# Attention's denominators: four sums an octet through a ring of four PSUM banks, instead of one accumulated sum in a bank of its own

## The reference

```python
attn = jax.nn.softmax(jnp.einsum('bhnd,bhmd->bhnm', q, k) * scale, axis=-1)
out = jnp.einsum('bhnm,bhmd->bhnd', attn, v)
out = out.transpose(0, 1, 3, 2).reshape(B, C, H, W)
out = conv1x1(out, wo, bo)
return (out + q_in) / jnp.sqrt(jnp.float32(2.0))
```

## Time and profile before

| | before |
|---|---|
| median of the runs shown | 5332.25 us |
| the profiled execution, its own time | 5332.55 us |
| its span, first to last instruction | 5330.8 us |
| PE busy | 5102.7 us, 96% of the span |
| DVE busy | 3992.7 us, 75% |
| POOL busy | 3101.9 us, 58% |
| ACT busy | 2791.8 us, 52% |
| mean granted clock of PE | 0.981 of full speed |

### The profile page before, as it was taken

One profiled execution on the slowest core, in us unless ns is written; L12 is line 12 of the kernel. 1 busy time (PEld: TensorE's weight loads), 2 busy tenths in 40 slices (PEclk: granted clock), 3 DMA queues, 4 the chain that ended last, 5 costly groups with the idle time before them and its releaser, 6 DMA issues. The chain is left out here.

```text
span 5330.8 us, 97583 instructions
## 1 busy us (share of the span) xinstructions
PE 5102.7 (96%) x31976; PEld 2498.0 (47%) x31976; DVE 3992.7 (75%) x5122; ACT 2791.8 (52%) x5168; POOL 3101.9 (58%) x1336
## 2 busy tenths in 40 slices
PE   6989999999999999999999999999978999999887
PEld 3434444444444444444444444444436655555333
DVE  3228888888888888888888888888835887677533
ACT  1114666666666666666666666666651334433401
POOL 0005888888888888888888888888850000000000
PEclk9997999999999999999999999999979999999998
DMA  3230010010100000000101010011121000000254
GB/s 152 94 116 20 11 28 23 13 26 12 28 23 16 24 20 19 26 14 23 28 11 28 11 26 25 13 26 43 41 96 54 12 31 22 31 22 25 81 160 158
DMA packets 97275, 217.89 MB, mean 41 GB/s; under 512 B 12848, under 2 KB 22192, under 8 KB 93616
## 3 DMA queue, kind: packets, MB, share of 16 engines
q1 hardware_dynamic: 96816, 211.85, 12.5%
HBM read 131.07 MB, written 80.22 MB: 40 GB/s over the span
## 5 line engine op out<-in xcount | busy, mean ns | idle before, releaser
L703 DVE TENSOR_REDUCE b_mx<-b_pmax 128x1 f32<-128x512 f32 x4096 | 2518.6, 682 | 499.6 <-PE b_pmax L533 495.1
L669 ACT ACTIVATE b_prob<-b_pscore 128x512 f32<-128x512 f32 x4096 | 2183.7, 609 | 1233.4 <-PE b_pscore L548 1225.0
L514 POOL TENSOR_TENSOR b_sums<-b_sums,b_prob 128x1024 f32<-128x1024 f32 x1024 | 2444.7, 2387 | 441.4 <-DVE b_sums L722 306.4
L533 PE MATMUL b_pmax<-b_kst,b_qst 96*128 96x512 f32 x4096 | 1849.3, 455 | 35.4 <-DMA b_qst<-scratch_ql 15.0
L548 PE MATMUL b_pscore<-b_qst,b_kst 98*128 98x512 f32 x4096 | 1644.6, 402 | 19.5 <-ACT b_prob L669 9.7
L533 PEld LDWEIGHTS b_pmax<-b_kst,b_qst 96*128 96x128 f32 x4096 | 776.5, 190 | 1088.2 <-DVE b_mx L703 740.0
L561 PE MATMUL b_pout<-b_prob,b_vst 128*32 128x512 f32 x8192 | 994.0, 603 | 0.0
L508 POOL TENSOR_TENSOR b_sums<-b_prob 128x1024 f32<-128x1024 f32 x256 | 607.9, 2375 | 453.2 <-ACT b_prob L669 448.3
L548 PEld LDWEIGHTS b_pscore<-b_qst,b_kst 98*128 98x128 f32 x4096 | 778.4, 190 | 144.1 <-ACT b_prob L669 56.1
L1337 DVE SCALAR_TENSOR_TENSOR d_dsum<-d_ypad,d_dw,d_dsum 128x2048 f32<-128x2048 f32 x288 | 681.7, 2367 | 10.2
L722 DVE TENSOR_TENSOR b_sums<-b_prob 128x1024 f32<-128x1024 f32 x256 | 475.6, 1858 | 49.0 <-ACT b_prob L669 49.0
(11 more groups left out here) (129 smaller groups left out, 2314.4 us busy)
## 6 DMA issues: line engine op xcount, KB each, us to landing
b_kst<-scratch_kh SPq DMA_DIRECT2D x32, 512.0 KB, 9.3
b_qst<-scratch_qh SPq DMA_DIRECT2D x128, 128.0 KB, 2.5
scratch_att<-b_outn SPq DMA_DIRECT2D x128, 128.0 KB
scratch_num<-d_num SPq DMA_DIRECT2D x64, 256.0 KB, 2.0
f_num<-scratch_num SPq DMA_DIRECT2D x8, 2048.0 KB, 10.1
f_rden<-scratch_rden SPq DMA_DIRECT2D x64, 256.0 KB, 9.4
a_x<-in_x SPq DMA_DIRECT2D x4, 2048.0 KB, 14.5
scratch_qh<-a_high SPq DMA_DIRECT2D x8, 1024.0 KB, 4.0
```

Source lines behind the costliest of these rows:

```text
L514: pool.tensor_tensor(acc, acc, p[:, step, :], ALU.add).then_inc(pool_added, 1)
L533: pe.matmul(pmax[max_bank(place_of(u, m))][:], qst[0:SUMS, b, t * P:(t + 1) * P], kst[0:SUMS, par, j * BANK:(j + 1) * BANK], start=True, s ...
L669: act.activation(prob[:, kt % PBUF, half * BANK:(half + 1) * BANK], pscore[score_bank(hs)][:], ACT.Exp, scale=SCALE).then_inc(exped, 1)
L703: dve.tensor_reduce(mx[:, b, t, j:j + 1], pmax[max_bank(place_of(u, m))][:], AX.X, ALU.max).then_inc(max_read, 1)
```

## The change

The bank `pden` goes, and the maxima's ring gets it: four banks instead of three. Each octet's denominators are now a sum of their own. They take the next place in the ring, between the third and the fourth maximum product of a pair, and ACT copies that bank after the first tile of the octet that follows (four copies a unit). SP stores each octet's two rows apart, `scratch_att_den` has eight rows a head instead of two, and the output stage loads eight and adds them in three steps. A list `USES` gives each use of the ring in a unit its place; 69 uses a unit are one more than a multiple of four, so the banks shift by one from unit to unit.

```diff
-        pmax = [pb(f"b_pmax{i}", [P, BANK]) for i in range(3)]
+        pmax = [pb(f"b_pmax{i}", [P, BANK]) for i in range(RING)]
         pout = pb("b_pout", [P, BANK])
-        pden = pb("b_pden", [P, BANK])
...
+        USES = []
+        for pair in range(PAIRS):
+            USES += [("max", PER_PAIR * pair + n, pair) for n in range(PER_PAIR - 1)]
+            if pair % (OCT // 2) == OCT // 2 - 1:
+                USES.append(("den", pair // (OCT // 2), pair))
+            USES.append(("max", PER_PAIR * pair + PER_PAIR - 1, pair))
+            if pair == PAIRS - EARLY:
+                USES.append(("turn", 0, pair))
+        PLACE = {use[:2]: j for j, use in enumerate(USES)}
+        def bank_of(c, kind, n):
+            return (c + PLACE[kind, n]) % RING
+        def await_read(eng, u, kind, n):
+            if kind == "max":
+                eng.wait_ge(max_read, maxima(AHEAD + u * MAXES + n + 1))
+            elif kind == "den":
+                eng.wait_ge(den_read, done(u * OCTS + n))
+            else:
+                eng.wait_ge(shift_low, done(u + 2))
+        def bank_free(eng, u, kind, n):
+            j = PLACE[kind, n] - RING
...
+                if not absent:
+                    return await_read(eng, u, kind, n)
...
-            def denominators(u, o):
-                if o == 0:
-                    pe.wait_ge(den_read, done(u))
+            def denominators(bank, u, o):
                 pe.wait_ge(pool_added, done((u * OCTS + o + 1) * ADDS))
...
-                        mm = pe.matmul(pden[row:row + 1, :], ones[:],
+                        mm = pe.matmul(pmax[bank][row:row + 1, :], ones[:],
                                        sums[:, o % 2, s, half * BANK:(half + 1) * BANK],
-                                       start=(o == 0), stop=(o == OCTS - 1))
+                                       start=True, stop=True)
...
-                            if o:
-                                denominators(u, o - 1)
-                            elif behind:
-                                denominators(u - 1, OCTS - 1)
+                            if o or behind:
+                                bank_free(pe, u, "den", o)
+                                denominators(bank_of(c, "den", o), u if o else u - 1, (o - 1) % OCTS)
...
-                act.activation(outd[:], pden[:], ACT.Copy).then_inc(den_read, 1)
+                act.activation(outd[:], pmax[bank][:], ACT.Copy).then_inc(den_read, 1)
...
-                    if behind and kt == OCT + 2:
-                        read_den(u - 1)
+                    if kt % OCT == 0:
+                        g = kt // OCT - 2
+                        if g >= 0 or behind:
+                            where = bank_of(c, "den", g + 1) if kt else bank_of((c - 1) % UNITS, "den", OCTS - 1)
+                            read_den(where, u if g >= 0 else u - 1, g % OCTS)
...
-            dve.memset(pden[:], 0.0).then_inc(consts, 1)
...
-            for s in range(2):
-                sp.dma_start(dens[:, s, :], scr.att_den[:, s, :].rearrange("h (a n) -> h a n", n=BANK)).then_inc(den_in, 16)
+            for s in range(8):
+                sp.dma_start(dens[:, s, :], scr.att_den[:, s // 2, s % 2, :].rearrange(
+                    "h (a n) -> h a n", n=BANK)).then_inc(den_in, 16)
...
-            dve.tensor_tensor(dens[:, 0, :], dens[:, 0, :], dens[:, 1, :], ALU.add).then_inc(chain, 1)
-            dve.wait_ge(chain, 1)
+            for step, half in enumerate((4, 2, 1)):
+                dve.tensor_tensor(dens[:, 0:half, :], dens[:, 0:half, :], dens[:, half:2 * half, :],
+                                  ALU.add).then_inc(chain, 1)
+                dve.wait_ge(chain, step + 1)
```

More of the change, by code:

```diff
@@ L381, in score_bank @@
             return 1 if hs == HS - 1 else hs % 3
[L383 to L404, removed]
-            else:
-                eng.wait_ge(max_read, maxima(u * MAXES + (there if there < T_AT else there - 1) + 1))
+        USES = []
@@ new lines, in await_start @@
+        def await_start(eng, j):
+            kind, n = START[j]
+            if kind == "max":
+                eng.wait_ge(max_read, maxima(n + 1))
+            else:
+                eng.wait_ge(shift_low, done(1))
+        def bank_free(eng, u, kind, n):
+            j = PLACE[kind, n] - RING
+            while True:
+                if j < 0:
+                    if is_unit(u, 0):
+                        return await_start(eng, j + len(START))
+                    u, j = u - 1, j + len(USES)
+                kind, n, pair = USES[j]
+                absent = (kind == "den" and n == 0 and is_unit(u, 0)
+                          or is_unit(u, ALL)
+                          or kind == "max" and (is_unit(u, ALL - 1) or is_unit(u, ALL - 2) and pair >= PAIRS - EARLY)
+                          or kind == "turn" and is_unit(u, ALL - 1))
+                if not absent:
+                    return await_read(eng, u, kind, n)
+                j -= RING
@@ L477, in turn @@
                     if not (first and place == 0):
-                        store(u - 1, head if c else head - 1, (c - 1) % UNITS)
+                        old = (u - 1, head if c else head - 1, (c - 1) % UNITS)
+                        store_den(*old, OCTS - 2)
+                        store(*old)
                     sp.wait_ge(scored, done(u * HS))
@@ L487, in turn @@
                         load_x(place - 2)
+                    if not (first and place == 0):
+                        store_den(*old, OCTS - 1)
+                    for o in range(OCTS - 2):
+                        store_den(u, head, c, o)
                     if not (final and place == TURN - 1):
@@ L580, in _ @@
             pe.wait_ge(k_in[0], done(48))
[L581 to L587, removed]
+            for j, (kind, n) in enumerate(START):
+                if j == MAXES:
+                    pe.wait_ge(q_in[1], done(48))
+                if j >= RING:
+                    await_start(pe, j - RING)
+                if kind == "turn":
+                    transpose_shift(start_bank(j), 0)
+                else:
+                    max_product(start_bank(j), n % MAXES, 0, n // MAXES)
             def turn(i, first, final):
@@ L604, in turn, with one_maximum @@
                                 pe.wait_ge(k_in[t_par], done((i + target // TURN + 1) * 48))
+                        def one_maximum(n):
+                            if products:
+                                bank_free(pe, u, "max", PER_PAIR * pair + n)
+                                max_product(bank_of(c, "max", PER_PAIR * pair + n), products[n], t_par, t_buf)
                         for part in range(4):
                             scores(u, 4 * pair + part, par, place % QBUF)
-                            for m in products[part:part + 1] if part < 3 else ():
-                                max_product(u + ahead, m, t_par, t_buf)
+                            if part < 3:
+                                one_maximum(part)
                         if pair % 2:
@@ L631, in _ @@
                 times_v(ALL - 1, HEADS - 1, 1, UNITS - 1, pair)
-            denominators(ALL - 1, OCTS - 1)
+            bank_free(pe, ALL, "den", 0)
+            denominators(bank_of(0, "den", 0), ALL - 1, OCTS - 1)
         @block.scalar
@@ L728, in _ @@
                 dve.memset(kst[SUMS:P, par, :].bitcast(F32), 1.0).then_inc(consts, 1)
[L729 to L735, removed]
+            for j, (kind, n) in enumerate(START):
+                if j == MAXES:
+                    top(0, 0)
+                if kind == "max":
+                    read_max(start_bank(j), n // MAXES, n % MAXES, n // MAXES)
+                if j == MAXES + T_AT + 1:
+                    low_shift(start_bank(MAXES + T_AT), 0)
             def turn(i, final):
@@ L751, in turn @@
                             if products:
-                                read_max(u + ahead, products[n], (place + ahead) % 2)
+                                read_max(bank_of(c, "max", PER_PAIR * pair + n), u + ahead, products[n], (place + ahead) % 2)
                             if n == 0 and pair == PAIRS - EARLY + 1 and shift:
-                                low_shift(u + 1)
+                                low_shift(bank_of(c, "turn", 0), u + 1)
             with dve.Fori(0, TURNS - 1) as i:
```

72 lines of the change are left out of this document (39 added, 33 removed).

## The result

The changed kernel takes 5385.6 us (median of 4 runs, 5378.0 to 5386.8), the kernel before in the same comparison 5331.1: ratio 1.0099, 95% interval 1.0084 to 1.0113, 1.0% slower. The forecast was 5384. The profiled span grew by 53.5 us, from 5330.8 to 5384.3.

What follows compares the result with a forecast made beforehand. PE was taken as the bound, with waits for banks of the maxima's ring. Net +0.73 us a unit times 62.7 units (+46), last unit +1.8 and output stage +4.1 gave +52 on 5332.25: 5384 us, range 5344 to 5435.

Steps and rivals of the forecast that it cites:

- The copy holds M3: Fourth maximum product (M3) of half A waits for ACT's copy of the denominators: 0.99 us later.
- half A: PE's work of two pairs following the denominators: 6.19 us before, forecast 6.78, four a unit.
- The fourth bank: Ring waits of plain halves go: half A alone would take 5.79 us, plain half B 6.66.
- Plain half B: PE's work of two pairs ending with the denominators, no maxima turned: 7.05 us before, forecast 6.66.
- turned half: The one half B a unit in which the maxima are turned: 8.17 us before, forecast 0.86 less.
- the half with the numerators' copy: One half B of each unit, where ACT holds a score product whatever the ring does: -0.08 us.
- Around it: Outside the units' halves: last unit +1.8 us for ACT's added copies, output stage +4.1 (bounds 0 and 8.2).
- Rival 1: The copy comes in time, M3 finds its bank free: 3.23 us won a unit, 5136 us; chance 0.07.
- POOL is no rival: Claim that POOL sets no bound: busy 696 of 800 us, and the octet gets no shorter.
- rival 2: About even: M3's delay 0.75 to 0.83, or the turned half wins 1.5; within 11 us of 5332; chance 0.07.
- Rival 3: Ring wins less or ACT's queue costs more: 5586 us without any fourth-bank gain, or 5474; chance 0.07.
- rival 4: PE's clock falls: times-V at twice its 1.85 us in 251 octets, +464, 5848 us; chance 0.02.

Runs made afterwards that it cites:

- e8: e1 without POOL's last addition of an octet (p7 left out of the sum): 5133.2 us, ratio 0.9626.
- e5: e1 with two of an octet's six additions in one DVE instruction, before POOL's four: 5153.8 us, ratio 0.9667.
- e6: The changed kernel with two of an octet's six additions in one DVE instruction, before POOL's four: 5383.1 us, ratio 1.0102.
- e9: e5 with the copy of the denominators behind one exponential: 5270.7 us, ratio 0.9879.
- e1: The changed kernel with ACT's copy of the denominators ahead of both exponentials instead of behind them: 5328.0 us, ratio 0.9981.
- e2: The changed kernel with the copy of the denominators behind one exponential instead of two: 5334.2 us, ratio 0.9990.
- e11: The changed kernel, copy behind two exponentials, with three banks in the ring instead of four: 5691.5 us, ratio 1.0669.
- e7: The kernel before with two of an octet's six additions in one DVE instruction, before POOL's four: 5327.9 us, ratio 0.9983.
- e3: The changed kernel with the copy of the denominators behind three exponentials instead of two: 5600.8 us, ratio 1.0496.

## Why the prediction was right

*The copy holds M3.* Predicted: the copy ends 2.34 after M0, M3 starts at 2.39, delay 0.99, half A 6.78. Measured 2.35, 2.40, and 6.795 against 5.795 in e8, so 1.00. e5, e6 and e9 show it is this wait. Its line, 294.6 at the weight loads, was foretold as 200 to 250. The 0.89 foretold for M3 itself was right, it starts 1.11 after S2 (2090.47 to 2091.58) instead of 0.234, so 0.88 late; the row of its weight load shows 1.16 because it counts from the end of the load before.

*The fourth bank.* Plain half B 6.66 foretold, 6.65 measured (median); turned half 7.31 and 7.31, with M5 at 2.74 for 2.72 and times-V at 4.60 for 4.59. A unit grew by 0.81 from transpose to transpose instead of 0.73: +51 for +46. Half of the 5 is the half with the numerators' copy, 7.01 instead of 6.97. The other half lies at the loop's turn, where the six long halves A take 59.6 us instead of 53.7; 6 x 0.59 = 3.5 more were counted.

*Around it.* The last unit was foretold at +1.8 and is 1.3 shorter from the last transpose to the last copy (66.05 and 64.80 us). The output stage, answering to the earlier trace rows:

```profile
3998.24 5.20 SPq L864 DMA_DIRECT2D c_dens<-scratch_att_den  x8
```

```profile
4008.97 4.28 DVE L960 TENSOR_TENSOR c_dens<-c_dens 128x2048 f32<-128x2048 f32 x3 [24.78 <-DMA c_dens<-scratch_att_den]
```

```profile
4017.84 1.91 ACT L921 ACTIVATE c_w_hi<-c_w 128x2048 fp32r<-128x2048 f32 x1 [4.39 <-DMA c_bo<-in_bo]
```

ACT still waits for the weights, and starts 25.05 us after the last copy instead of 21.92: +3.1 for +4.1. These misses, +5, -3 and -1, cancel: that the total came within 2 us is luck, that the half A and the turned half did is not.

*What was wrong lies in the rivals.* Rival 1 priced a copy in time at 5136 us; e1 took 5328. The step that failed is "POOL is no rival: it is busy 696 of 800 us in rows 2, and the octet gets no shorter". That holds for the forecast but not for rival 1 or for rival 2's even point, where the octet does get shorter. I read POOL's busy share and not its gaps: most of what was not busy was POOL waiting for DVE's addition, 306 us over the kernel before, so it had no room:

```profile
L514 POOL TENSOR_TENSOR b_sums<-b_sums,b_prob 128x1024 f32<-128x1024 f32 x1024 | 2444.7, 2387 | 441.4 <-DVE b_sums L722 306.4 <-POOL b_sums L514 61.4 <-ACT b_prob L669 42.4
```

With the additions freed, e8 at 5133 meets the 5136 and e5 at 5154 comes near it. Rival 2's rule, a gain once M3's delay falls under 0.81, fails the same way: e2, with a delay near 0.5, gains 0.1%; e9, freed, gains 1.2%. Rival 3's 5586 for a ring without gain was too low, e11 took 5691: half A is 7.41 where 6.19 + 0.99 = 7.18 was counted, and much of the rest is rival 4, the clock. The forecast kernel escapes it but for the loop's turn; a longer wait does not.

## What to carry to other kernels

A result that goes into a shared ring holds a bank for as long as its reader's queue says: put the read ahead of the work that it needn't follow, or the bank becomes a wait at its next use. When a wait is taken away, look for the engine whose gaps are themselves waits for another: its busy share shows room that is not there. Two bounds may lie at the same pace, and each then hides what the other is worth until both are moved (e1 and e7 0.2% each, e5 3.3%).

## What the hardware showed

DVE's and POOL's additions of two operands in SBUF did not run side by side. Over all of an octet's additions in e1 the time of DVE's one is 1.08 us plus the time for which one of POOL's lies beside it (5th to 95th percentile of the difference 1.08 to 1.09 us); on the mean it is 3067 ns in e1, 1858 before, 1276 in the changed kernel, by phase alone. With none of POOL's beside it, it takes 1.21 us (median in e8). POOL's keep their 2.38 (median) throughout, but for the few that started second, while DVE's was under way: the five in e1, all after the last transpose, took about 3.13. The Trainium skill's "SBUF — State Buffer" (Who interferes with whom) says that a VectorE instruction with two inputs in SBUF contends with a GpSimd instruction that reads SBUF, over shared ports that are an exclusive lock, and that issue order decides who blocks. The trace agrees: DVE's addition above, which started second, was blocked for 2.27 of its 3.35 us, and POOL's were held when they started second.

PE's clock: with waits of M3 as in the changed kernel (0.75 us on PE on the mean, 250 times) the granted clock stayed at 1.00 in every half A outside the loop's turn, up to the last unit. In e3 and e11, with waits of 1.2 on the mean, about one half A in six ran partly at the lower level (44 and 41 of 250, 0.81 on the mean of the half); the clock fell close to M3's start or up to 2 us behind it. At the loop's turn it fell in some halves of either kernel, by one profiled execution of each.
